# A weight quantiser's step split in two stages, with its quotient on GpSimd and its subtract as two operations

## What is computed

```python
def ternary_quant(w_fp32, g=64):
    w = w_fp32.astype(bfloat16)
    w_g = w.reshape(-1, g)
    scale = clip(mean(abs(w_g), axis=-1, keepdims=True), 1e-08, None)
    q = clip(round(w_g / scale), -1, 1)
    return (q * scale).reshape(w.shape)        # value used in the forward pass

def block(x):                                  # x: [4, 2048, 2048] fp32
    xn = layernorm(x)
    # attention: 16 heads of 128, causal, Wq/Wk/Wv/Wo [2048, 2048] fp32
    attn = softmax(mask(q @ k.T / sqrt(128))) @ v @ Wo + bo
    # feed-forward: w_gate_up [16384, 2048], w_proj [2048, 8192] fp32
    gate, up = split(xn @ ternary_quant(w_gate_up).T)
    h = silu(gate) * up
    ffn = rms_norm(h) @ ternary_quant(w_proj).T
    return x + attn + ffn
```

## Time and profile before

| | us |
|---|---|
| median of 3 runs (lowest to highest) | 5871.64 (5812.32 to 5905.2) |
| profiled execution | 5863.48 |
| span of its slowest core (core 5) | 5861.9 |
| spans of the other cores | 5785.1 to 5841.2 |
| busy on core 5: PE, DVE, ACT, POOL | 3054.0, 2527.4, 493.2, 273.6 |

### The profile page before, as it was taken

The page is one execution under the profiler, slowest core; times in us unless marked ns, Lnnn a source line. Parts: engine busy times, 40 slices in busy tenths (PEclk is TensorE's granted clock), DMA queues, the critical chain, the costliest instruction groups (busy, mean ns, idle before and its releaser), DMA issues.

```text
span 5861.9 us, 33491 instructions; the slowest of 8 cores (5785.1 to 5861.9 us)
## 1 busy us (share of the span) xinstructions
PE 3054.0 (52%) x11224; PEld 1115.3 (19%) x11224; DVE 2527.4 (43%) x2055; ACT 493.2 (8%) x560; POOL 273.6 (5%) x524
## 2 busy tenths in 40 slices
PE   0073333332664443444434429777776667777655
PEld 0031111111221110101101003233322223333222
DVE  5405777774888777767777741011110011110000
ACT  2110000000000221211111110000000000000000
POOL 0000000000000000000000000010100000111000
PEclk9996666766787666666666667899999989997999
DMA  5616555557556444455554551333235543222455
GB/s 150 156 29 128 120 126 125 122 125 121 131 130 140 117 114 111 104 104 108 104 111 98 109 105 62 108 102 107 101 126 182 198 153 108 101 101 90 161 198 182
DMA packets 767647, 713.31 MB, mean 122 GB/s; under 512 B 632179, under 2 KB 640500, under 8 KB 760308
## 3 DMA queue, kind: packets, MB, share of 16 engines
q0 software_dynamic: 74880, 276.86, 21.7%
q1 hardware_dynamic: 406134, 237.15, 13.9%
q10 hardware_dynamic: 286464, 197.16, 11.7%
HBM read 597.82 MB, written 134.22 MB: 125 GB/s over the span
## 4 chain that ended last, share of the span: by engine, by line
DMA 34%; DVE 29%; PE 28%; issue 5%; ACT 3%; DVEq 1%; ACTq 0%; SPq 0%; POOL 0%; POOLq 0%
PE PS L765 9%; PE PS L770 8%; DMA wpT<-wptdram 8%; DVE qm L400 7%; DVE qb L403 7%; DMA qquot<-qb 6%; DMA qm<-qb 5%; DVE qquot L392 5%; PE PS L850 5%; DMA wgqt<-qquot 3%; DMA wgqt<-qm 3%; PE PS L698 2%; DMA wptdram<-qquot 2%; DVE qm L397 2%; PE PS L321 2%
## 5 line engine op out<-in xcount | busy, mean ns | idle before, releaser
L765 PE MATMUL PS<-XT_own,wT 128*128 128x512 bf16 x2048 | 841.5, 411 | 32.7 <-DVE ost L880 16.6
L770 PE MATMUL PS<-XT_own,wT 128*128 128x512 bf16 x2048 | 838.1, 409 | 0.0
L850 PE MATMUL PS<-wpT,Hbig 128*128 128x512 bf16 x2048 | 500.8, 390 | 273.6 <-DMA wpT<-wptdram 240.6
L392 DVE TENSOR_TENSOR qquot<-qb,qgr 128x2048 bf16<-128x2048 bf16 x192 | 440.2, 2293 | 408.0 <-DMA wgqt<-qquot 236.6
L785 DVE TENSOR_TENSOR Hbig<-silu_sb,PS 128x512 bf16<-128x512 bf16 x128 | 88.0, 688 | 1193.5 <-ACT silu_sb L781 1193.5
L619 PE MATMUL PS<-Pt,onc 128*1 128x512 bf16 x512 | 195.4, 472 | 731.8 <-ACT Pt L607 730.7
L379 DVE TENSOR_REDUCE qgs<-qb 128x32 f32<-128x2048 bf16 x192 | 438.5, 2284 | 260.5 <-DMA qb<-wgu 245.8
L400 DVE SCALAR_TENSOR_TENSOR qm<-qquot,qm 128x2048 bf16<-128x2048 bf16 x192 | 440.1, 2292 | 21.0 <-DVE qm L397 1.4
L403 DVE TENSOR_TENSOR qb<-qm,qgs 128x2048 bf16<-128x2048 bf16 x192 | 440.1, 2292 | 21.0 <-DVE qm L400 1.4
L880 DVE SCALAR_TENSOR_TENSOR ost<-PS,invcol,acct 128x2048 f32<-128x2048 f32 x8 | 18.8, 2351 | 771.5 <-PE PS L850 738.9
L466 PE MATMUL PS<-XT_own,Wsb 128*128 128x512 bf16 x512 | 148.6, 456 | 338.0 <-ACT kvst L477 277.2
(11 more groups left out here) (69 smaller groups left out, 2269.2 us busy)
## 6 DMA issues: line engine op xcount, KB each, us to landing
wT<-wgqt POOLq DMA_DIRECT2D x256, 512.0 KB, 4.7
wpT<-wptdram ACTq DMA_DIRECT2D x256, 512.0 KB, 3.3
qb<-wgu POOLq DMA_DIRECT2D x128, 512.0 KB, 6.6
wgqt<-qquot SPq DMA_DIRECT2D x64, 512.0 KB, 2.8
wgqt<-qm SPq DMA_DIRECT2D x64, 512.0 KB, 2.8
qb<-wp POOLq DMA_DIRECT2D x64, 512.0 KB, 7.3
Xf<-x_kv SPq DMA_DIRECT2D x16, 1024.0 KB, 5.2
wptdram<-qquot SPq DMA_DIRECT2D x32, 512.0 KB, 4.0
```

Source lines behind the costliest of these rows:

```text
L392: t5 = P.op("dve", (lambda e, b=b: e.tensor_tensor(qquot[:, :].rearrange("p (g s) -> p g s", s=64), b[:, :].rearrange("p (g s) -> p g s", ...
L765: e.matmul(PS[:, (gb + rh) * 512:(gb + rh) * 512 + w], wT[par * 2][:, k * 128:(k + 1) * 128], XT_own[:, k * TQ + scol0 + rh * 512: k * TQ ...
L770: ii = e.matmul(PS[:, (2 + rh) * 512:(2 + rh) * 512 + w], wT[par * 2 + 1][:, k * 128:(k + 1) * 128], XT_own[:, k * TQ + scol0 + rh * 512: ...
L850: ii = e.matmul(PS[:, sc * 2048 + dt * 512: sc * 2048 + (dt + 1) * 512], Hbig[:, k * SHALF + row * 128: k * SHALF + row * 128 + 128], wpT[ ...
```

## The change

`step` is cut into `_stage_a` (t1 to t5) and `_stage_b` (t6 to t8, transpose, store, and the load of tile i+2). A call emits stage A of one tile and then stage B of the tile before it; `finish` emits what is left. The small tiles `qgs`, `qgc`, `qgr` and the tile `qquot` exist twice, by parity; `qm2` is gone, and `qpt` is the pair `qquot`. t5 moves from DVE to POOL, with a semaphore of its own. t7 was one scalar_tensor_tensor; it is now a tensor_scalar (t7a, `> 0.5` in place in `qquot[par]`) and a tensor_tensor subtract, and t6 writes its result into `qb[par]`. t5 waits only for the store from its own `qquot[par]`. SBUF use for the big tiles is the same: two `qb` and two `qquot` where there were two `qb`, `qquot` and `qm2`. The diff, cut to its core:

```diff
-    qquot = at("qquot", [128, D], BF16, o=KA0 + 2 * D * 2)
-    qm2 = at("qm2", [128, D], BF16, o=KA0 + 3 * D * 2)
-    qpt = [qquot, qm2]
+    qquot = [at("qquot%d" % i, [128, D], BF16, o=KA0 + (2 + i) * D * 2)
+             for i in range(2)]
+    qpt = qquot
...
+        def _stage_a(self, i):
+            par = i % 2
+            b = qb[par]
...
+            if i not in self.load_tok:
+                self._load(i)
+            t1 = P.op("dve", (lambda e, b=b, par=par: e.tensor_reduce(
+                qgs[par][:, 0:ng],
...
+                deps=[self.load_tok[i]] + self.chain[par])
...
+            self.t5_tok[i] = P.op(
+                "pool", (lambda e, b=b, par=par: e.tensor_tensor(
+                    qquot[par][:, :].rearrange("p (g s) -> p g s", s=64),
+                    b[:, :].rearrange("p (g s) -> p g s", s=64),
+                    qgr[par][:, 0:ng].unsqueeze(2).broadcast_to(
+                        [128, ng, 64]),
+                    AL.mult)), deps=[t4, self.qpt_st[par]], sem="pl")
+
+        def _stage_b(self, i):
...
+            t6 = P.op("dve", (lambda e, b=b, par=par: e.tensor_scalar(
+                b[:, :], qquot[par][:, :], -0.5, None, AL.is_lt)),
+                deps=[self.t5_tok[i]])
+            t7a = P.op("dve", (lambda e, par=par: e.tensor_scalar(
+                qquot[par][:, :], qquot[par][:, :], 0.5, None, AL.is_gt)),
+                deps=[t6])
+            t7 = P.op("dve", (lambda e, b=b, par=par: e.tensor_tensor(
+                b[:, :], qquot[par][:, :], b[:, :], AL.subtract)),
+                deps=[t7a])
+            t8 = P.op("dve", (lambda e, b=b, par=par: e.tensor_tensor(
...
+            self.chain[par] = [t8]
...
+            tp = P.dma(tq_eng, tq_sem,
...
+                       deps=[t8, self.qpt_st[par]])
+            self.last[tq_sem] = tp
+            self.buf_free[par] = [tp]
...
+            self.qpt_st[par] = ts_
+            self.last["dqs%d" % par] = ts_
+            if i + 2 < self.n:
+                self._load(i + 2)
+
         def step(self, k=1):
             for _ in range(k):
-                if self.i >= self.n:
-                    return
-                i = self.i
-                self.i += 1
-                for j in (i, i + 1):
-                    if j < self.n and j not in self.load_tok:
-                        self._load(j)
...
-                t5 = P.op("dve", (lambda e, b=b: e.tensor_tensor(
...
-                    AL.mult)), deps=[t4, self.qpt_st[0]])
-                t6 = P.op("dve", (lambda e: e.tensor_scalar(
-                    qm2[:, :], qquot[:, :], -0.5, None, AL.is_lt)),
-                    deps=[t5, self.qpt_st[1]])
-                t7 = P.op("dve", (lambda e: e.scalar_tensor_tensor(
-                    qm2[:, :], qquot[:, :], 0.5, qm2[:, :],
-                    AL.is_gt, AL.subtract)), deps=[t6])
...
+                if self.ia < self.n:
+                    self._stage_a(self.ia)
+                    self.ia += 1
+                if self.ib < self.ia - 1:
+                    self._stage_b(self.ib)
+                    self.ib += 1
```

More of the change, by code:

```diff
@@ L181, in build_nc @@
     qb = [at("qb%d" % i, [128, D], BF16, o=KA0 + i * D * 2) for i in range(2)]
-    qquot = at("qquot", [128, D], BF16, o=KA0 + 2 * D * 2)
-    qm2 = at("qm2", [128, D], BF16, o=KA0 + 3 * D * 2)
-    qpt = [qquot, qm2]
+    qquot = [at("qquot%d" % i, [128, D], BF16, o=KA0 + (2 + i) * D * 2)
+             for i in range(2)]
+    qpt = qquot
     QG0 = TOP0 + 2 * 1024 * 2
[L186 to L189, removed]
+    qgs = [at("qgs%d" % i, [128, D // 64], F32, o=QG0 + i * 128)
+           for i in range(2)]
+    qgc = [at("qgc%d" % i, [128, D // 64], BF16, o=QG0 + 256 + i * 64)
+           for i in range(2)]
+    qgr = [at("qgr%d" % i, [128, D // 64], F32, o=QG0 + 384 + i * 128)
+           for i in range(2)]
+    assert QG0 + 640 <= SB
     o = W0
@@ L344, in __init__ @@
             self.n = self.N_GU + self.N_WP
-            self.i = 0
+            self.ia = 0
+            self.ib = 0
             self.load_tok = {}
-            self.buf_free = [[qbig_done], [qbig_done2]]
-            self.chain = [qbig_done]
+            self.buf_free = {0: [qbig_done], 1: [qbig_done2]}
+            self.chain = {0: [qbig_done], 1: [qbig_done2]}
             self.qpt_st = [qbig_done, qbig_done2]
+            self.t5_tok = {}
             self.last = {}
@@ L364, in _load @@
             self.last["dga%d" % par] = self.load_tok[i]
+        def _stage_a(self, i):
+            par = i % 2
+            b = qb[par]
+            ng = D // 64
+            if i not in self.load_tok:
[3 more added lines that the diff above has]
+                b[:, :].rearrange("p (g s) -> p g s", s=64),
+                AX.X, AL.add, apply_absolute_value=True)),
+                deps=[self.load_tok[i]] + self.chain[par])
+            t2 = P.op("dve", (lambda e, par=par: e.tensor_scalar(
+                qgc[par][:, 0:ng], qgs[par][:, 0:ng], 1.0 / 64, None,
+                AL.mult)), deps=[t1])
+            t3 = P.op("dve", (lambda e, par=par: e.tensor_scalar(
+                qgs[par][:, 0:ng], qgc[par][:, 0:ng], 1e-8, None, AL.max)),
+                deps=[t2])
+            t4 = P.op("dve", (lambda e, par=par: e.reciprocal(
+                qgr[par][:, 0:ng], qgs[par][:, 0:ng])), deps=[t3])
+            self.t5_tok[i] = P.op(
+                "pool", (lambda e, b=b, par=par: e.tensor_tensor(
+                    qquot[par][:, :].rearrange("p (g s) -> p g s", s=64),
+                    b[:, :].rearrange("p (g s) -> p g s", s=64),
+                    qgr[par][:, 0:ng].unsqueeze(2).broadcast_to(
+                        [128, ng, 64]),
+                    AL.mult)), deps=[t4, self.qpt_st[par]], sem="pl")
@@ new lines, in _stage_b, with stg, stw @@
+        def _stage_b(self, i):
+            par = i % 2
+            b = qb[par]
+            ng = D // 64
+            t6 = P.op("dve", (lambda e, b=b, par=par: e.tensor_scalar(
[8 more added lines that the diff above has]
+            t8 = P.op("dve", (lambda e, b=b, par=par: e.tensor_tensor(
+                b[:, :].rearrange("p (g s) -> p g s", s=64),
+                b[:, :].rearrange("p (g s) -> p g s", s=64),
+                qgs[par][:, 0:ng].unsqueeze(2).broadcast_to([128, ng, 64]),
+                AL.mult)), deps=[t7])
+            self.chain[par] = [t8]
+            tq_eng, tq_sem = (("act", "dqt0") if par == 0
+                              else ("sync", "dqt1"))
+            tp = P.dma(tq_eng, tq_sem,
+                       (lambda e, b=b, par=par: e.dma_start(
+                           out=qpt[par][:, :].rearrange(
+                               "p (k r) -> p k r", k=DB),
+                           in_=b[:, :], transpose=True)),
+                       deps=[t8, self.qpt_st[par]])
+            self.last[tq_sem] = tp
+            self.buf_free[par] = [tp]
+            if i < self.N_GU:
+                def stg(e, i=i, par=par):
+                    return e.dma_start(
+                        out=wgqt[i * 128:(i + 1) * 128, :],
+                        in_=qpt[par][:, :])
+                ts_ = P.dma("sync", "dqs%d" % par, stg, deps=[tp])
+            else:
+                t, sub = (i - self.N_GU) // (FFH // D), (i - self.N_GU) % (FFH // D)
+                def stw(e, t=t, sub=sub, par=par):
+                    dst = wptdram[sub * D:(sub + 1) * D,
+                                  t * 128:(t + 1) * 128]
+                    dst = dst.rearrange("(k p) r -> p k r", p=128)
+                    return e.dma_start(
+                        out=dst, in_=qpt[par][:, :].rearrange(
+                            "p (k r) -> p k r", k=DB))
+                ts_ = P.dma("sync", "dqs%d" % par, stw, deps=[tp])
+            self.qpt_st[par] = ts_
+            self.last["dqs%d" % par] = ts_
+            if i + 2 < self.n:
+                self._load(i + 2)
@@ L384, in step @@
[L384 to L391, removed]
-                t5 = P.op("dve", (lambda e, b=b: e.tensor_tensor(
-                    qquot[:, :].rearrange("p (g s) -> p g s", s=64),
-                    b[:, :].rearrange("p (g s) -> p g s", s=64),
-                    qgr[:, 0:ng].unsqueeze(2).broadcast_to([128, ng, 64]),
-                    AL.mult)), deps=[t4, self.qpt_st[0]])
@@ L435, in step @@
-                self.qpt_st[ip] = ts_
-                self.last["dqs%d" % ip] = ts_
-        def finish(self):
-            while self.i < self.n:
-                self.step(1)
-            return [t for t in self.last.values()] + self.chain
+                if self.ia < self.n:
[4 more added lines that the diff above has]
+                    self.ib += 1
+        def finish(self):
+            while self.ia < self.n:
+                self._stage_a(self.ia)
+                self.ia += 1
+            while self.ib < self.n:
+                self._stage_b(self.ib)
+                self.ib += 1
+            return [t for t in self.last.values()] + \
+                self.chain[0] + self.chain[1]
```

9 lines of the change are left out of this document (removed).

## The result

| | before | after |
|---|---|---|
| median of 10 runs (lowest to highest), us | 5867.96 (5802.04 to 5989.27) | 7536.41 (7496.3 to 7691.71) |
| profiled execution, us | 5863.48 | 7530.85 |
| spans of the cores, us | 5785.1 to 5861.9 | 7424.2 to 7529.2 |
| granted clock, mean of a core | 0.782 to 0.801 | 0.725 to 0.733 |

The ratio is 1.2918, 95% interval 1.2855 to 1.2982. The time lies in the forecast range; the profiled execution is 289 us under the forecast point. Any of these kernels has executions in which the cores of a die show a lower granted clock and the time is some per cent longer; the ratios, and the column "undisturbed" further down, leave them out.

What follows compares the result with a forecast made beforehand. Quantiser steps on DVE pace K, V and attention. The serial load adds 1112 us to 5863.5 (K +384, K to V +5, V +184, attention +539), giving 6975; the turns add 845: 7820 us. Range 6900 to 8050.

Steps and rivals of the forecast that it cites:

- The order uncovers the load: Quantiser: with two buffers, DVE waits 11.2 us for transpose, issue and load after each B; period 19.9 against 13.76 us.
- the queues: ScalarE's queue (K evacuations, exponentials, so PE) and SP's (K and V stores) wait behind the transposes and follow DVE's period.
- The turns: POOL's quotient and DVE's stage B alternate on SBUF, adding 4.4 us a step, +845 us; forecast with serial load, chance 0.58.
- the operation that would show it: In stage B, most likely the one behind is_lt, lasting or waiting about 4 us longer while POOL's quotient runs.
- the cited rule: Trainium skill: DVE instructions in 2-port mode or with two SBUF inputs and a GpSimd instruction reading SBUF exclude each other.
- The quotient's price: POOL's 128x2048 quotient, taken as 4.4 us: its two inputs read one after the other; lower bound 2.29.
- The memset ratio: Alternative price for POOL's quotient: 128x1 memset takes 98 ns on POOL, 59 on DVE, giving 3.8 us.
- K to V: Change of stage: Wv loads stand in POOL's queue behind load(64); between 0 and +9 us, taken as +5.
- V's evacuation: V stage, 32 steps of 19.86 us: the evacuation falls into the wait for the load; stage +184 us.
- The subtract: Stage B on DVE: three bf16 operands, 2048 columns, 1.24 us taken; bounds 1.24 and 2.29.
- The head's tail: Attention, after a head's sixth call: three exponentials and the last matmuls before DVE's reciprocal, 9.3 us, 16 times 149 us.
- O and FFN: O projection and FFN, after the heads: the same program, change 0.

Runs made afterwards that it cites:

- e2: The changed kernel with POOL's quotient cut to 64 of 2048 columns from the third tile on: 6963 us, 1.189 of the kernel before.
- e4: The changed kernel with a third load buffer, its order and POOL quotient kept: 5636 us, 0.950 of the kernel before.
- e1: The changed kernel with one tile per call (stage A, next load, stage B), quotient still on POOL: 5676 us, 0.969 of the kernel before.
- e3: The changed kernel with the quotient back on DVE, order and two buffers kept: 7509 us, 1.277 of the kernel before.
- e7: The changed kernel with two extra DVE reduces into a scratch tile between stages A and B: 7925 us, 1.344 of the kernel before.
- e8: The changed kernel with four load buffers, POOL's quotient held until the previous tile's stage B ends, transposes on swapped queues: 5190 us, 0.874 of the kernel before.
- e9: Control for e8: four load buffers, but one tile per call and the quotient on DVE: 5311 us, 0.909 of the kernel before.

## Why the prediction was right, point by point

- **The order uncovers the load: shown, both ways.** 175 waits behind the first against 175 forecast, 11.3 us each in K against 11.2. With the turns gone (e2) the step is 19.88 against 19.86; with one more buffer (e4) or the old order (e1) the step is back under 13.76. What was forecast of the queues held too: ScalarE and PE follow the same period.
- **The turns: shown** (e2, e3, e7 and the last tile). The prediction could give them no row and took them at 0.58. That choice was right, and the operation that would show it was named. The reason given beside the cited rule, that both engines move whole 128x2048 tiles at the same time, was not: the reduce reads a whole tile beside the quotient and keeps its 2.29 (e7), and a 128x32 scaling is held (e8).
- **The quotient's price was the term that was off.** 4.4 us was taken, 3.80 measured, 3.61 where nothing meets it. The memset ratio of the earlier trace rows, set aside for having no inputs, had given 3.8; that a 128x1 memset gave the nearer number is luck, since no run shows why it should.
- **A turn costs less than the quotient.** The sum charged 4.4 a call. The comparison grew by 3.2 (3.89 for 0.69): POOL starts 0.3 us before `< -0.5` is done, and the comparison ends 0.54 us after the quotient, less than its own 0.69. 192 x 1.2 = 230 of the 289 us, from the price and the shorter turn together.
- **The rest, some 60 us:** B starts 0.08 us before A's reciprocal is over instead of 0.11 after it, and its first operation takes 0.63 for 0.69 (0.25 a call, -48 in all); K to V -13; outside the quantiser +24 and -52 with the clock. Against it V's evacuation, taken as wholly hidden in the wait: e2 has 20.62 a step in V for 19.88 in K, +24.
- **The subtract:** 1.23 against 1.24.
- **The head's tail** of 9.3 us before the reciprocal was close: DVE idles 9.54 there in the last head, and 8.4 to 9.7 in the others. **O and FFN** kept their work; their length moved with the clock alone.

## What to carry to other kernels

Before a stage is put one tile ahead, read the queue in order and count the buffers: a load that is issued behind the consumer's last read has only what stands between that and the next use for its cover; one tile ahead wants one buffer more (here 1900 us for 4 KB a partition). Before an operation goes to GpSimd, look which VectorE operations will stand beside it: here, next to a tensor_scalar or tensor_tensor on SBUF tiles, most of it was added to VectorE's own time (3.2 of 3.8 us), and next to a reduce nothing was. Both together took this kernel from 1.29 to 0.87; the buffers with the quotient on DVE and one tile per call (e9) had 0.91.

## What the runs showed of the hardware that I had not expected

- POOL's 128x2048 quotient takes 3.61 us alone and up to 5.7 (in e4, where DVE operations are under way when it starts); a 128x32 tensor_scalar of 0.18 us on DVE is held for up to 3.4 us beside it (3.60 in all, in e8).
- The same 512 KB load lands in a median of 5.8 us in e1 and 6.6 in the kernels before and after. In e1 it is issued 3.6 us behind the start of the last store instead of 0.5 (medians in K), so the two meet less; no run separates this from other causes.
- The granted clock differed between executions in stretches with the same work: 0.84 and 0.92 in the Q projection, worth 22 us. What set it, no run here tells.
